# Layer 1 experts: from all experts on all rows to sorted blocks of chosen rows, with the routing done inside the self-attention

## What is computed

```python
x = x + _L1_attn_ref(_layernorm(x), L1_attn_gamma, L1_attn_w_qkv, L1_attn_w_out)
x = x + _L1_ffn_ref(_layernorm(x), L1_ffn_gate_W, L1_ffn_W1, L1_ffn_b1, L1_ffn_W2, L1_ffn_b2)

def _L1_ffn_ref(x, gate_W, W1, b1, W2, b2):       # 8 experts, 128 -> 256 -> 128
    logits = x_flat @ gate_W
    gates = softmax(logits)
    tk_g, tk_i = top_k(gates, 2)
    tk_g = tk_g / (sum(tk_g) + 1e-08)
    cw = sum(one_hot(tk_i, E) * tk_g[..., None], axis=1)
    out = x_flat
    for e in range(E):
        h = relu(x_flat @ W1[e] + b1[e])
        out = out + cw[:, e:e + 1] * (h @ W2[e] + b2[e])
    return out
```

## Time and profile before

| | us |
|---|---|
| median of 3 runs | 1725.85 |
| lowest and highest | 1720.89, 1728.99 |
| the profiled execution's own time | 1724.12 |
| its span, first to last instruction | 1722.3 |

### The profile page before, as it was taken

One profiled execution on the slowest core, in us unless ns is written; L12 is line 12 of the kernel. 1 busy time (PEld: TensorE's weight loads), 2 busy tenths in 40 slices (PEclk: granted clock), 3 DMA queues, 4 the chain that ended last, 5 costly groups with the idle time before them and its releaser, 6 DMA issues. The chain is left out here.

```text
span 1722.3 us, 46099 instructions
## 1 busy us (share of the span) xinstructions
PE 1506.3 (87%) x15538; PEld 1145.9 (67%) x15538; DVE 1078.3 (63%) x3391; ACT 853.4 (50%) x2372; POOL 531.7 (31%) x1145
## 2 busy tenths in 40 slices
PE   3887888857889699999999999789999999599998
PEld 2666666646567566666666666567777777488887
DVE  3888888846310267777777777656666666333333
ACT  2555555521233267777777777534444444144443
POOL 1444444420714334444444444422222222000000
PEclk9999999975889889999999999999999999699999
DMA  5455633200111211111111111000000000000000
GB/s 186 162 168 168 228 117 104 81 1 0 51 38 49 76 35 34 34 34 34 33 33 33 33 33 34 13 1 0 0 0 0 0 0 1 1 7 12 6 12 12
DMA packets 67039, 80.26 MB, mean 47 GB/s; under 512 B 8422, under 2 KB 54643, under 8 KB 66864
## 3 DMA queue, kind: packets, MB, share of 16 engines
q1 hardware_dynamic: 64848, 76.06, 14.7%
q0 software_dynamic: 2144, 3.60, 0.7%
HBM read 69.52 MB, written 10.91 MB: 47 GB/s over the span
## 5 line engine op out<-in xcount | busy, mean ns | idle before, releaser
L1621 ACT ACTIVATE c_pr<-c_pS,c_nm 128x257 f32<-128x257 f32 x512 | 238.2, 471 | 97.5 <-DVE c_nm L1755 97.5
L1755 DVE TENSOR_REDUCE c_nm<-c_pS 128x1 f32<-128x257 f32 (+1 forms) x384 | 173.2, 505 | 42.7 <-PE c_pS L1501 42.4
L1995 ACT ACTIVATE s_k<-s_pK 128x512 f32<-128x512 f32 x128 | 76.4, 597 | 177.3 <-PE s_pK L1922 177.3
L1505 PE MATMUL c_pT<-cst,c_pr 128*128 128x128 f32 x1024 | 163.2, 284 | 0.0
L1375 ACT ACTIVATE f_hid<-f_pH,vec 128x512 f32<-128x512 f32 x128 | 88.0, 687 | 128.5 <-PE f_pH L1337 127.2
L1397 DVE SCALAR_TENSOR_TENSOR X<-f_pY,f_mk,X 128x128 f32 x256 | 72.1, 344 | 111.6 <-PE f_pY L1347 111.6
L1922 PEld LDWEIGHTS s_pK<-s_hT,AH 128*128 128x128 f32 x1024 | 124.0, 195 | 25.9 <-ACT s_k L1995 22.8
L1922 PE MATMUL s_pK<-s_hT,AH 128*128 128x128 f32 x1024 | 137.7, 284 | 0.5 <-ACT s_hT L1990 0.5
L1505 PEld LDWEIGHTS c_pT<-cst,c_pr 128*128 128x128 f32 x1024 | 111.4, 141 | 37.7 <-issue 37.7
L1347 PEld LDWEIGHTS f_pY<-f_w,f_hid 128*128 128x128 f32 x1024 | 122.3, 192 | 5.1
L1347 PE MATMUL f_pY<-f_w,f_hid 128*128 128x128 f32 x1024 | 124.1, 276 | 0.0
(11 more groups left out here) (300 smaller groups left out, 3188.5 us busy)
## 6 DMA issues: line engine op xcount, KB each, us to landing
a_ctxT<-in_ctxT SPq DMA_DIRECT2D x32, 514.0 KB, 3.7
c_ctxT<-in_ctxT SPq DMA_DIRECT2D x128, 128.5 KB, 2.2
a_ctxN<-in_ctxR SPq DMA_DIRECT2D x32, 512.0 KB, 4.1
f_w<-in_f_w SPq DMA_DIRECT2D x16, 256.0 KB, 3.3
rows_in<-a_zero SPq DMA_DIRECT2D x7, 322.5 KB, 4.3
f_h<-rows_in SPq DMA_DIRECT2D x7, 322.5 KB
a_ctxL<-in_ctxL SPq DMA_DIRECT2D x128, 16.0 KB, 3.5
f_w<-in_f_w SPq DMA_DIRECT2D x16, 128.0 KB, 3.3
```

Source lines behind the costliest of these rows:

```text
L1505: mm = pe.transpose(pT[:, c, j, :], pr[:, b % 2, j, c * P:(c + 1) * P], k("ident"))
L1621: act.activation(pr[:, b % 2, c, :], pS[:, c, 0:S], ACT.Exp, bias=nm[:, c:c + 1], accum_out=den[:, b % 2, c:c + 1]).then_inc(e_ready.sem, 1)
L1755: dve.tensor_reduce(nm[:, c:end], pS[:, c:end, 0:S], AX.X, ALU.max, negate=True).then_inc(max_ready.sem, 1)
```

## The change: what it does

- **Room and constants.** Layer 1 gets a DRAM table `rows1_in` with a region of 4096 rows for each expert. A row has 130 numbers: 128 values, the number of its destination, and its gate weight. First choices fill a region from its start, second choices from its end. During the cross-attention SP fills the table with blanks, one 532 KB write in each of the 32 groups, from a tile that POOL sets at the start of that stage.
- **Routing inside the self-attention.** The slots are arranged as 5 single ones, a loop of 6 times 4, and 3 single ones. For each batch of 4 groups DVE picks the first and second expert (`choose`, 12 operations), computes weights and running counts (`weigh`, 12 operations) and destinations (`place`, 4 operations); ACT does one small exponential; PE counts ranks with four products of 32 columns (`ranks`), whose result shares the bank of the scores. The last 4 groups are two batches of 2. POOL copies each group's rows twice into `HH` and scatters them with two indirect transfers per group, from the ninth slot on, two groups in each of the last four slots. The split copies of the turned rows (`HT_parts`) go, and so does the stage `gate_layer1`.
- **Experts on blocks.** All first choices, sorted by expert, need at most 39 blocks of 128 rows whatever the routing, and so do the second choices: 78 blocks always run. A table computed at the stage's start gives each block's first row and its expert. Each block is one transfer from DRAM, a turn on PE, 2 matmuls up, relu, 2 matmuls down, a scaling by the gate weight, and an indirect scatter of 128 rows to `rows1_out`. SP, PE and DVE each read the block's row or expert number into a register first (`value_load`). DVE copies the block's w1 into a small buffer. The matmuls are on plain float32 instead of the three-part products.
- **Bias and end.** The b2 term is added for 8 groups at a time at the stage's start. First choices are gathered and added from block 47 on, second choices at the end, then the result is stored.

The diff, cut to what the stages do (the code of `choose` and `weigh` is 24 small dependent DVE operations and is shortened):

```diff
+BLOCKS = (TOKENS + E * (P - 1)) // P
+RB = 4
...
-        gate_layer1(env)
         experts_layer1(env)
...
 def experts_layer1(env):
...
+            sp.wait_ge(rows_ready, 2)
+            sp.wait_ge(scattered, 16 * 2 * G)
+            for i in range(TOTAL):
+                if i == A_FROM:
+                    gather(0, BLOCKS)
+                start = sp.value_load(row_i[0:1, i:i + 1], min_val=0, max_val=E * TOKENS - P)
+                if i >= RB:
+                    sp.wait_ge(y_ready, i - RB + 1)
+                sp.dma_start(hb[:, i % RB, :], rows_in[bass.ds(start, P), :]).then_inc(h_loaded[i % RB], 16)
+            gather(1, TOTAL)
...
+            def turn(i):
+                pe.wait_ge(h_loaded[i % RB], 16 * (i // RB + 1))
+                if i > 1:
+                    pe.wait_ge(hT_ready, i - 1)
+                pe.transpose(pT[:, i % 2, 0:P], hb[:, i % RB, 0:D], k("ident")).then_inc(hT_done, 1)
+            def up(i):
+                pe.wait_ge(hT_ready, i + 1)
+                pe.wait_ge(w1b_ready, i + 1)
+                if i > 1:
+                    pe.wait_ge(up_ready, NF * (i - 1))
+                for c in range(NF):
+                    mm = pe.matmul(pH[...], w1b[...], hT[:, i % 2, :], start=True, stop=True)
+                mm.then_inc(up_done, 1)
+            def down(i):
+                e = pe.value_load(expert_i[0:1, i:i + 1], min_val=0, max_val=E - 1)
+                pe.wait_ge(up_ready, NF * (i + 1))
+                if i > 1:
+                    pe.wait_ge(y_ready, i - 1)
+                for c in range(NF):
+                    mm = pe.matmul(pY[:, i % 2, 0:D], hid[:, i % 2, c, :], w2[:, bass.ds(e, 1), c, :]...)
+                mm.then_inc(down_done, 1)
...
+            turn(0)
+            turn(1)
+            up(0)
+            for i in range(TOTAL):
+                if i + 2 < TOTAL:
+                    turn(i + 2)
+                if i + 1 < TOTAL:
+                    up(i + 1)
+                down(i)
...
+            def weights(i):
+                e = dve.value_load(expert_i[0:1, i:i + 1], min_val=0, max_val=E - 1)
+                if i > 1:
+                    dve.wait_ge(up_done, i - 1)
+                dve.tensor_copy(w1b[:, i % 2, :], w1[:, bass.ds(e, 1), :]...).then_inc(w1b_ready, 1)
+            def outputs(i):
+                dve.wait_ge(down_done, i + 1)
+                if i >= RB:
+                    dve.wait_ge(y_scattered[i % RB], 16 * (i // RB))
+                dve.tensor_scalar(yb[:, i % RB, :], pY[:, i % 2, 0:D], hb[:, i % RB, D + 1:D + 2], None, ALU.mult).then_inc(y_ready, 1)
...
+            for i in range(TOTAL):
+                if i + 2 < TOTAL:
+                    weights(i + 2)
+                    tokens(i + 2)
+                outputs(i)
+                if i >= A_FROM + 3 and (i - A_FROM) % A_EVERY == 0 and (i - A_FROM) // A_EVERY <= NB:
+                    add(0, (i - A_FROM) // A_EVERY - 1)
+            for n in range(NB):
+                add(1, n)
...
 def cross_layer1(env):
+                sp.wait_ge(blank_ready.sem, 2)
+                sp.dma_start(regions[bass.ds(g, 1), :, :, :].rearrange("g p k d -> p (g k) d"), blank[:, :, :]).then_inc(env["rows1_zeroed"], 16)
...
 def self_layer1(env):
+                if j == (2 if isinstance(b, int) else 3):
+                    pe.wait_ge(places.sem, places.at(b, 1))
                 scores(g, p)
...
                 sums(g, p)
+                if j == (1 if isinstance(b, int) else 2):
+                    ranks(b)
                 if not last:
                     keys(g + 1, 1 - p, (2, 3))
...
+                if j == (1 if isinstance(b, int) else 2):
+                    place(b)
                 if not first:
+                    if not early(g, 2):
+                        dve.wait_ge(rows_kept.sem, rows_kept.at(g - 2))
                     n6.vector_scale(dve, x_of(g - 1), g - 1)
```

More of the change, by code:

```diff
@@ L1952, in logits, with ranks, slot @@
                 pe.matmul(pM[:, 2, 0:E], h5T[:, :], gate[:, :], start=True, stop=True).then_inc(lg_done.sem, 1)
-            def slot(g, p, first, last, norm):
+            def ranks(b):
+                n = batch(b)[1]
+                hot = of_batch(hot_all, b)
+                pe.wait_ge(hot_ready.sem, hot_ready.at(b))
+                pe.wait_ge(tally.sem, tally_at(b, n))
+                for c in range(2):
+                    below, all_ = (k("before"), k("ones")) if c == 0 else (minus[:, 0, :], minus[:, 1, :])
+                    pe.matmul(pR[:, 0:n, c, :], below, hot[:, :, c, :], start=True, stop=False)
+                    mm = pe.matmul(pR[:, 0:n, c, :], all_, earlier[:, 0:n, c, :], start=False, stop=True)
+                mm.then_inc(rank_done.sem, 1)
+            def slot(g, p, first, last, norm, j, b):
                 if not last:
@@ L2160, in _ @@
             keep_logits(G - 2)
+            weigh(7)
             add_output(G - 1)
@@ L2166, in _ @@
             keep_logits(G - 1)
+            choose(8)
+            weigh(8)
+            place(8)
 def kernel(**inputs):
```

537 lines of the change are left out of this document (359 added, 178 removed).

## The result

The changed kernel took 1738.69 us (median of 4 runs, 1737.79 to 1743.25), the kernel before 1725.95 beside it: a ratio of 1.0087, 95% interval 1.007 to 1.0105. It is slower by 0.9%, where 0.8% faster was forecast. The span of the profiled execution went from 1722.3 to 1736.0 us.

The account below looks back on a forecast made before the run. PE was taken to bound self-attention and the old experts, the ring of four loads the new blocks. Terms +1.5, +2, +14, -6.1 and -25.4 (new experts 208.5 against 233.9) gave -14: median 1712 us, 8-in-10 range 1682 to 1746.

Parts of the forecast that it names:

- Cross-attention, +1.5: Cross-attention: POOL's filling before its first norm costs 1.5 us, bounds 0 and 4; loads behind the blanking writes stay early.
- Self-attention, +16: Self-attention: +2 us at the start for constants and small POOL work, +14 for seven batches at 2.0 each.
- two times 0.5: Self-attention, per batch: `choose` and `weigh`, 2.4 us each on DVE against 1.6 free, each cost PE 0.5 us.
- the ranks' 0.9: Self-attention, per batch: the four `ranks` products, counted as 8 matmul instructions, cost PE 0.9 us in full.
- Rival C: Self-attention: waits and address instructions make `choose`, `weigh`, `place` cost PE 4 us a batch; term +28, time 1726; chance 0.12.
- Join, -6.1: Self-attention's end to experts: 12.2 us become 4.9 of chained DVE operations plus a 1.2 barrier, 6.1 us less.
- Experts' start, 16: Start of experts: table ready at 7.8 us, DVE's four bias additions until 15, first block at 16 (12 to 20).
- Rival B: Experts' blocks: PE stays at the lower clock, period 2.45 us, blocks 191, time 1735 if throughout; chance 0.13.
- Blocks, 168 + 8: Experts: 78 blocks at 2.15 us give 168; the gather at block 47 and DVE's additions add 8.
- two periods are one pass and one way: Blocks, ring of four loads: PE's pass 1.7 plus 2.6 from down(i) to turn(i+4), halved, gives a 2.15 us period.
- Rival D: Blocks: the ring of four loads does not bind; period about 1.55 us, blocks 121, time 1665; chance 0.1.
- End, 16.5: Experts' end: scaling 0.5, scatter 1.1, landing 1.1, gathers and additions 10.5, store 3.3; 16.5 us (14 to 20).

Follow-up runs that it names:

- experiment 1: Changed kernel with the gates' exponential on ACT issued one slot later, behind slot 1's softmax exponential: 1722.09 us, 1.0047 of the kernel before.
- experiment 15: experiment 9 with DVE's work on a batch spread over the four slots, rank products in slot 3, scatters one slot later: 0.9834 of the kernel before.
- experiment 8: Changed kernel with the four products that rank a batch's rows issued twice: 1.0148 of the kernel before.
- Experiment 5: Changed kernel with exponential moved, four more scatters in the experts' stage, GpSimd's last self-attention wait removed so its DRAIN starts early: 1.0031 of the kernel before.
- Experiment 2: Changed kernel with the term gates times b2 left out of the experts' stage: 1.0016 of the kernel before.
- experiment 3: Changed kernel with eight buffers in place of four for loaded blocks and results: 1677.89 us, 0.9779 of the kernel before.
- experiment 16: experiment 9 with DVE's work spread evenly over slots, early register load, split bias, spread gather, end on two queues: 1689.77 us, 0.9816 of the kernel before.
- experiment 6: Changed kernel with moved exponential, early DRAIN, eight buffers, b2 in the block loop, spread gather, end on two queues: 0.9853 of the kernel before.
- experiment 9: Changed kernel with moved exponential, early DRAIN and eight buffers together, nothing else: 0.9875 of the kernel before.
- experiment 10: experiment 9 with PE's register load moved from ahead of the second product to the start of the block's turn: 0.9869 of the kernel before.
- experiment 11: experiment 9 with first choices gathered one transfer every two blocks from load 51, last gathers and stores on two queues: 0.9841 of the kernel before.
- experiment 12: experiment 9 with one of four b2 rounds ahead of the blocks and three behind the last block: 0.9838 of the kernel before.
- experiment 4: Changed kernel with the scatters of groups 28 and 29 moved to the experts' start, eight there instead of four: 1.0084 of the kernel before.
- experiment 13: The kernel of experiment 3, unchanged, run again on another chip: 0.9915 of the kernel before.

## Why the prediction was wrong

*What bounds.* Right: PE binds in the self-attention, and in the new experts it is not last any more.

*Cross-attention, +1.5.* -0.2 measured: GpSimd's filling and the 17 MB of blanks are hidden.

*Self-attention, +16.* This step failed, 27.2 measured: the price of a batch, 3.7 us and not 2.0. It was built from DVE's and PE's own lengths (0.9 and two times 0.5). Right was the length of `choose`. Missed was a third engine: the exponential was counted as nothing, and its wait in ACT's in-order queue costs 0.78 a batch (experiment 1). Undersized was what DVE takes beyond its slack: 1.7 a batch in slots 0 and 1, where two times 0.5 was taken (experiment 15). Of the ranks' 0.9, 0.44 is shown as late work (experiment 8); the slot with them costs 1.18. Rival C had the size (28) at a chance of 0.12, by small waits of DVE; this was its outcome, but in part by ACT's queue. About 0.7 of the 3.7 us, in the slot with the ranks, has no shown cause.

*Join, -6.1.* -1.7 measured: 0.8 from longer chained steps and 3.6 from GpSimd's DRAIN, which the forecast took as the old barrier of 1.2. Experiment 5 shows it. The trace of before had such a row: the DRAIN at the end of layer 0's experts took 10.3 us (576.1 to 586.4), of which 5.5 lie behind the end of GpSimd's last indirect transfer, under the cover of other engines.

*Experts' start, 16.* 25.7 measured. The step that failed took PE's part of the bias as nearly covered by DVE's additions (1.4 each, 1.23 measured), while PE needs 5.65 a round at the lower clock. Experiment 2 gives 12 us for the chain. Rival B was right to fear the lower clock after the join, and wrong on where it costs: the steady blocks ran at 0.98.

*Blocks, 168 + 8.* 172.0 measured, nearly right, and partly by luck: two periods are one pass and one way was right in form, but the pass is 1.43 with the register load at 0.48 (experiment 3, another chip), not 1.7 at 0.75. The way, worked out from a period of 2.07, is then 2.7 (2.6 forecast), an estimate. The gather's stall of 6.7 was forecast as 6 to 8. Rival D's 1.55 is what eight buffers give (1.53 with the gather).

*End, 16.5.* 20.2 measured. From the first gather's issue to the last addition 10.3 us pass (10.5 forecast), and 3.4 ahead of it (2.7). The mis-sized term is the store: 6.5 us from the last addition to the end (1729.5 to 1736.0) in place of 3.3, with eight stores issued over 7.4 us.

*The sum.* -14 forecast, +9 without the unchanged layer: 11 from the self-attention, 4.4 from the join, 9.7 from the start, 3.7 from the end, less 4 for the blocks and 1.7 for the cross-attention. All misses but two went one way: at the joins, and in work on ACT, GpSimd and PE that was counted as free or covered. The 4.4 us of layer 0 come on top and have nothing to do with the change. The measured 1738.7 lies inside the range of 1682 to 1746, but that width was meant for the register load and the clock in the blocks, and the miss came from other terms: that it covers the result is luck.

## What to carry to other kernels

A small instruction added to an idle engine is not free: look at what stands behind it in that engine's queue and how late its input is, and put it behind the instruction whose wait already covers it. Before work is moved across a stage's end, find in the trace how long each engine's DRAIN takes, and let the one with indirect transfers get there first. And where a loop alternates between a short and a long period, as here 1.8 and 2.3 us, the short one need not be the pass of the engine (1.43): try more buffers before pricing anything else.

## What the runs showed of the hardware

GpSimd's DRAIN at the end of a stage is long where GpSimd has issued indirect transfers in that stage, and 0.03 to 0.93 us in stages without them. Counted from its start or from the end of the last transfer's instruction, whichever is later, it goes with how many such transfers the stage has issued: 5.04 us after 54 (experiments 15, 16), 5.20 after 56 (5, 6 and 9 to 12), 5.40 after 60 (the changed kernel and the other experiments), 5.54 after 67 (layer 0's experts), 6.77 after 82, 7.09 after 86 and 7.26 after 88 (layer 1's experts). Only experiment 4, with 56, the last of them 12 us old, falls out of line (4.63). So four transfers fewer shorten it by some 0.2 us, and starting it early hid 3.7. What it does in this time is not shown.

A register load from on-chip memory took 0.27 to 0.31 us and the register work behind it 0.17 on PE and SP (0.21 on DVE), on PE's path in full. PE was busy for 24.5 of 26 us from 1518 to 1544, by the profile, with the small products of the bias term for the most part, and its clock stood at 0.50 all this time; in experiments 10 and 13 the same code had 6.8 us of it at full clock.

The same kernel with eight buffers ran on one chip at 1.43 us a block and on another, with stalls of 1.3 us every second or third block, at 1.8. With four buffers the median block took 2.0 to 2.1 us in all six profiles.
